# Attention chunk sums on VectorE: the three steps behind a chunk's sum are spread over the next two maxima

## Chip, cores, metric

One core of one Trainium2 chip. The metric is the device time of one execution in microseconds (us).

## What is computed

A block of three layers on x (2 batches, 256 tokens, width 256): cross attention onto a context of 4096 tokens, self attention, and a mixture of experts. The change lies in the cross attention. Its core, in the reference:

```python
qh = (q @ w_q).reshape(B, L, N_HEAD, D_HEAD).transpose(0, 2, 1, 3)
kvp = c @ w_kv
k, v = (kvp[..., :D_HEAD], kvp[..., D_HEAD:])
attn_score = jnp.einsum('bhid,bjd->bhij', qh, k) / np.sqrt(D_HEAD)
attn_prob = jax.nn.softmax(attn_score, axis=-1)
out = jnp.einsum('bhij,bjd->bhid', attn_prob, v)
out = out.transpose(0, 2, 1, 3).reshape(B, L, D)
return out @ w_concat
```

There are 16 heads of width 16, and one K and V for all of them. The context serves as both halves of the keys, so that every key counts twice, which leaves the softmax as it is over 4096 keys.

## The kernel before

The 2 x 16 x 256 rows of queries are cut into 16 chunks of 512 (two heads of one batch each); chunks 0 to 7 are batch 0. In the main loop chunk g goes through 32 steps s of 128 keys. At each step TensorE makes a block of transposed scores (line 574, into one of three banks), and ScalarE takes its exponential into Pb (line 962). Every four steps TensorE multiplies Pb with V (line 585) and adds it up in the bank ACC, whose 17th column of each head is the denominator. For the softmax the greatest score of each row is needed ahead of the exponentials: while chunk g is worked on, TensorE also makes the scores of chunk g+1 in the other orientation (line 568), 1024 keys wide, in a pair of banks pairS0 or pairS1. One pair is filled over two steps (an even one and the odd one behind it), and VectorE takes its maximum (row_max, line 1170) into mxp. After 16 pairs VectorE takes the maximum over them (mneg, line 1178), GpSimd splits it in two parts (mparts), and TensorE and ScalarE put it into qparts (the "rows" of lines 554 and 939).

The pairs are a ring of two. A turn number counts every use of it (MAX_TURN); TensorE waits ahead of turn n until max_free has counted n - 1, so until the use of two turns before is released. VectorE waits on max_filled.

The sums of chunk g - 1 take a turn of this ring, at step 12 of chunk g (SUMS_AT). ScalarE has saved ACC to SBUF; TensorE transposes it into the pair whose turn it is (line 593), and VectorE does three steps (sums_rows, lines 1184 to 1188): it adds the four quarters to osum, takes the reciprocal of the denominators (oden), and multiplies the two into O. Each of the first two is waited for by the next with the semaphore dve_chain (Chain.step), and the third one's end counts max_free up. The turn behind it is the maximum of step 12 of the same chunk, in the other pair; the turn after that, at step 14, fills again the pair that held the sums.

Other work is placed between steps by a table (BETWEEN): "qs" (the rows of queries of a later chunk, lines 545 and 546) at step 14 in chunks 6 to 13, ahead of that step's scores; and in chunks 0 to 4 the preparation of batch 1 at steps 8, 15 and 22. In chunk 2 that of step 15 is the projection of half a context (line 517), whose high part ScalarE takes (kvh) and whose low part VectorE takes (kvl, low_part, line 1165). SIDES_AT says at which steps the products with V come: step 20 and 21 have none. In chunk 15 there are no maxima left; batch 0 is closed there (close_T(0) transposes O at step 2), and batch 1 behind the loop. The sums of chunk 15 go through bank0 there (line 1258) and count o_done up, for which close_T(1) waits.

The engines run in order, each its own queue; SyncE issues all DMAs. The loop of chunks is written out by the program, without a planner.

Of the kernel before, what the change touches and what calls it, by code (L numbers as in the profile page):

```python
# [8 lines left out]
ALU = mybir.AluOpType  # L9
ACT = mybir.ActivationFunctionType  # L10
AX = mybir.AxisListType.X
# [11 lines left out]
XH, XD = 16, 16  # L23
KT = S // P
CW = 512
NCH = XH * L // CW
NBLK = CW // P
# [23 lines left out]
SUMS_AT = 12  # L51
# [10 lines left out]
NCHUNK = B * NCH  # L62
# [21 lines left out]
def pair_at(g, s):  # L84

    n = (g * KT + s) // 2
    return AHEAD_OF[n] if n < len(AHEAD_OF) else None


def turns():  # L90

    exp_turn, max_turn = {}, {}
    for what in PRO:
        ring = max_turn if what[0] == "max" else exp_turn
        ring[what] = len(ring)
    for g in range(NCHUNK):
        for s in range(KT):
            if s == SUMS_AT and g:
                max_turn["sums", g - 1] = len(max_turn)
            for what in BETWEEN.get((g, s), ()):  # L100
                exp_turn[what] = len(exp_turn)
            exp_turn["s", g, s] = len(exp_turn)
            if s % 2 == 0 and pair_at(g, s):
                max_turn[("max", *pair_at(g, s))] = len(max_turn)
    return exp_turn, max_turn


EXP_TURN, MAX_TURN = turns()
# [42 lines left out]
def build(nc, x, ctxT, w_q, w_kv, w_cat, w_qk, w_v, b_qkv, w_out, b_out, gate_wT, gate_b, w_up, w_down, out):  # L151
    with ExitStack() as stack:
# [3 lines left out]
        def sem(name):  # L156
            return stack.enter_context(nc.semaphore(name))

        bank = [stack.enter_context(nc.psum_tensor(f"bank{i}", [P, 512], F32)) for i in range(4)]
        pairS = [stack.enter_context(nc.psum_tensor(f"pairS{i}", [P, 1024], F32)) for i in range(2)]  # L160
# [47 lines left out]
        with ExitStack() as cross:  # L208
            def xb(name, shape, dt=F32):
                return cross.enter_context(nc.sbuf_tensor(name, shape, dt))  # L210
# [10 lines left out]
            osum = xb("osum", [P, NBLK, XD + 1])  # L221
# [7 lines left out]
            oden = xb("oden", [P, NBLK])  # L229
# [18 lines left out]
        max_filled, max_free = sem("max_filled"), sem("max_free")  # L248
# [8 lines left out]
        mparts_ready = sem("mparts_ready")  # L257
        pv_done = sem("pv_done")
        acc_saved, accT_ps = sem("acc_saved"), sem("accT_ps")
        o_done, oT_ps, oT_done, y_ps = sem("o_done"), sem("oT_ps"), sem("oT_done"), sem("y_ps")  # L260
        q_ps, k_ps, v_ps = sem("q_ps"), sem("k_ps"), sem("v_ps")
        q_moved, k_moved, v_moved = sem("q_moved"), sem("k_moved"), sem("v_moved")
# [193 lines left out]
        def _(pe):  # L456
            mm, tr = nc.tensor.matmul, nc.tensor.transpose

            def batch_T(src, b, dst):

                for k in range(KD):
                    for t in range(2):
                        last = tr(dst[:, k * L + t * P:k * L + (t + 1) * P],
                                  src[:, 2 * b + t, k * P:(k + 1) * P], ident[:])
                return last
# [130 lines left out]
            def close_T(b):  # L596
                if b == 0:
                    pe.wait_ge(max_free, MAX_TURN["sums", NCHUNK - 2])
                else:
                    pe.wait_ge(o_done, 1)  # L600
                batch_T(O, b, OFF[:, 0:512] if b == 0 else bank[1]).then_inc(oT_ps, 1)

            def close_product(b):
# [20 lines left out]
            for g in range(NCHUNK):  # L624
                for s in range(KT):
                    if s == SUMS_AT and g:
                        sums(g - 1, max_bank(("sums", g - 1))).then_inc(max_filled, 1)
                    if s == 2 and g == NCHUNK - 1:
                        close_T(0)
# [136 lines left out]
            sums(G - 1, bank[0]).then_inc(accT_ps, 1)  # L766
            begin_out(ACC)
            close_T(1)
            pe.wait_ge(v_moved, 2)
            attn_scores(0)  # L770
# [27 lines left out]
            n = NCYC  # L798
# [303 lines left out]
        def _(dve):  # L1102
            ch = Chain(dve, dve_chain)
# [27 lines left out]
            def close(b):  # L1131
                dve.wait_ge(y_ps, b + 1)
                add_batch(b, OFF[:, 512:1024] if b == 0 else MISC[:])
                layer_norm(range(2 * b, 2 * b + 2))

            def oT_move():
                dve.wait_ge(oT_ps, 1)
                CP(xnT[:, :, 0:L], OFF[:, 0:512].rearrange("p (k n) -> p k n", k=KD)).then_inc(oT_done, 1)

            def high(dst, full, here, done):  # L1140

                dve.wait_ge(here, 16)
                CP(dst[:], full[:]).then_inc(done, 1)
# [7 lines left out]
            def x_parts(src):  # L1151
                dve.wait_ge(xnT_ps, 1)
                CP(xh[:, :, 0:L], src.rearrange("p (k n) -> p k n", k=KD)).then_inc(xh_done, 1)
                x_low(0, src)

            def low_part(what):
                n = EXP_TURN[what]
                if what[0] == "qT":
                    m, cols = what[1], slice(what[2] * L, (what[2] + 1) * L)
                    dst, high, src = ql[:, m, cols], qh[:, m, cols], EXP[n % 3][:, 0:L]  # L1160
                else:
                    i = (2 * what[1] + what[2]) % 2
                    dst, high, src = kvl[:, i, :], kvh[:, i, :], EXP[n % 3][:]
                dve.wait_ge(exp_free, n + 1)
                TT(dst, src, high.bitcast(F32), ALU.subtract).then_inc(low_done, 1)

            def row_max(c, blk, kp):
                n = MAX_TURN["max", c, blk, kp]
                dve.wait_ge(max_filled, n + 1)
                nc.vector.reduce_max(mxp[:, c % 2 * NBLK + blk, kp:kp + 1], pairS[n % 2][:], AX).then_inc(max_free, 1)  # L1170
                if (blk, kp) == (NBLK - 1, NPAIR_K - 1):
                    block_max(c, n)

            def block_max(c, n):
                dve.wait_ge(max_free, n + 1)
                if c >= 2:
                    dve.wait_ge(mparts_ready, c - 1)
                nc.vector.tensor_reduce(out=mneg[:, c % 2, :], in_=mxp[:, c % 2 * NBLK:(c % 2 + 1) * NBLK, :],  # L1178
                                        op=ALU.max, axis=AX, negate=True).then_inc(mneg_ready, 1)

            def sums_rows(g, src, done):
                b, c = g // NCH, g % NCH
                quarters = src.rearrange("p (i k c) -> p i c k", i=NBLK, k=4)
                ch.step(nc.vector.reduce_sum(osum[:], quarters[:, :, 0:XD + 1, :], AX))
                ch.step(nc.vector.reciprocal(oden[:], osum[:, :, XD]))
                den = oden[:].rearrange("p (h t o) -> p h t o", t=2, o=1)
                dst = O[:, 2 * b:2 * b + 2, c * 2 * XD:(c + 1) * 2 * XD].rearrange("p t (h d) -> p h t d", h=2)
                TT(dst, osum[:, :, 0:XD].rearrange("p (h t) d -> p h t d", t=2), den.broadcast_to([P, 2, 2, XD]),
                   ALU.mult).then_inc(done, 1)

            dve.wait_ge(x_in, 16)
            layer_norm(range(0, 2))
# [15 lines left out]
            for g in range(NCHUNK):  # L1208
                for s in range(KT):
                    if s == 2 and g == NCHUNK - 1:  # L1210
                        oT_move()
                        for i in range(2):
                            high(wAh[i], wA[i], wA_in[i], wA_hi)
                        close(0)
                        for i in range(2):
                            high(wVh[i], wV[i], wV_in[i], wV_hi)
                    if s == 20 and g == NCHUNK - 1:
                        x_parts(OFF[:, 0:512])
                        TS(bq8[:], bqkv[:, 0, :], 1.0 / np.sqrt(AD), None, ALU.mult).then_inc(bq_done, 1)
                    if s == SUMS_AT and g:  # L1220
                        n = MAX_TURN["sums", g - 1]
                        dve.wait_ge(max_filled, n + 1)
                        sums_rows(g - 1, pairS[n % 2][:, 0:512], max_free)
                    for what in BETWEEN.get((g, s), ()):
                        if what in HALVED:
                            low_part(what)
                    if s % 2 == 0 and pair_at(g, s):
                        row_max(*pair_at(g, s))


            PJ, SB = [half[0], half[1]], [half[2], half[3]]
# [23 lines left out]
            dve.wait_ge(late_in, 16 * 6)  # L1255
            k_move(0, first, 1, PJ[1])
            dve.wait_ge(accT_ps, 1)
            sums_rows(NCHUNK - 1, bank[0][:], o_done)
            row_max(0)
            row_max(1)  # L1260
            reciprocals(0)
# [18 lines left out]
            n = NCYC  # L1280
# [161 lines left out]
```

## Time and profile before

| | us |
|---|---|
| median of 3 runs | 633.71 |
| lowest and highest | 627.2, 636.61 |
| the profiled execution | 633.59 |
| its span, first to last instruction | 631.8 |
| TensorE busy | 582.3 |
| VectorE busy | 465.1 |
| ScalarE busy | 410.4 |
| GpSimd busy | 118.3 |

PE is TensorE's matmuls, PEld its weight loads, DVE is VectorE, ACT is ScalarE, POOL is GpSimd. Times count from the start of the span. In a timeline each row has the start, the duration, the engine, the line, the operation and the tiles, output first; in brackets stands the idle time of the engine just before the row and what ended it, where there was some to tell of. Matmul ends are modelled. The chunk loop runs from about 50 to 414 us, the sums of chunk g - 1 in chunk g at 80.8 us for g = 1 to 405.5 us for g = 15; the last sums follow at 420.7 us.

### The profile page before, as it was taken

How to read it: one execution, taken by the hardware profiler on the slowest of the kernel's cores; microseconds unless marked ns; L12 is line 12 of the kernel's file. 1: busy time of each engine (PE TensorE's matmuls, PEld its weight loads, DVE VectorE, ACT ScalarE, POOL GpSimd, SP SyncE). 2: the span in 40 equal slices, each digit the busy share in tenths (PEclk: the TensorE clock that was granted, in tenths of full speed). 3: DMA queues.
4: the chain of work that ended last, by engine and by line, in shares of the span. 5: the costliest groups of instructions: out<-in, count | busy, mean ns of one | idle time of the engine just before them, and what ended most of it. 6: DMA issues, size and time to landing. Idle time of an engine off the chain costs nothing.

```text
span 631.8 us, 11892 instructions
## 1 busy us (share of the span) xinstructions
PE 582.3 (92%) x4512; PEld 322.6 (51%) x4512; DVE 465.1 (74%) x685; ACT 410.4 (65%) x834; POOL 118.3 (19%) x150
## 2 busy tenths in 40 slices
PE   3798999999999999999999998998999987789995
PEld 1363443444444444444444443466766655678885
DVE  6787887887999999899899994625545556584554
ACT  1347887888888887888888788654555540543451
POOL 4000000000000000000000001302355440357873
PEclk9999999999999999999999999899999997898998
DMA  8640001000000000000000000100001000122321
GB/s 316 245 142 1 2 1 32 37 3 1 1 2 2 1 2 1 2 2 1 1 3 1 1 1 2 34 1 1 25 26 43 17 5 5 58 84 75 100 83 34
DMA packets 11381, 21.99 MB, mean 35 GB/s; under 512 B 1858, under 2 KB 6724, under 8 KB 10308
## 3 DMA queue, kind: packets, MB, share of 16 engines
q1 hardware_dynamic: 11332, 21.31, 10.0%
q8 instruction: 34, 0.56, 0.4%
q14 instruction: 15, 0.12, 0.1%
HBM read 20.78 MB, written 0.52 MB: 34 GB/s over the span
## 4 chain that ended last, share of the span: by engine, by line
PE 73%; DVE 15%; ACT 5%; issue 4%; DMA 2%; POOL 1%; SPq 0%; DVEq 0%
PE bank L574 21%; PE bank L585 16%; DVE mxp L1170 11%; PE pairS L838 6%; PE pairS L663 5%; PE bank L855 4%; PE pairS L713 3%; ACT Pb L962 2%; PE bank L738 2%; PE bank L724 2%; PE bank L517 1%; PE pairS L824 1%; PE pairS L568 1%; DMA ctx<-ctxT 1%; PE pairS L593 1%
## 5 line engine op out<-in xcount | busy, mean ns | idle before, releaser
L1170 DVE TENSOR_REDUCE mxp<-pairS 128x1 f32<-128x1024 f32 x256 | 306.7, 1221 | 36.1 <-PE pairS L568 34.9
L962 ACT ACTIVATE Pb<-bank 128x512 f32<-128x512 f32 x512 | 274.0, 599 | 56.4 <-PE bank L574 43.8
L574 PE MATMUL bank<-qparts,kparts 64*128 64x512 f32 x512 | 189.7, 453 | 12.9 <-DVE mxp L1170 6.4
L568 PE MATMUL pairS<-kparts,qparts 64*128 64x512 f32 x512 | 189.3, 455 | 2.8 <-DVE mxp L1170 2.0
L585 PE MATMUL bank<-Pb,V 128*32 128x256 f32 x2048 | 151.6, 389 | 1.2 <-ACT accS L948 1.2
L574 PEld LDWEIGHTS bank<-qparts,kparts 64*128 64x128 f32 x512 | 78.6, 184 | 117.2 <-ACT Pb L962 75.5
L585 PEld LDWEIGHTS bank<-Pb,V 128*32 128x32 f32 x2048 | 46.5, 108 | 74.4 <-issue 47.5
L568 PEld LDWEIGHTS pairS<-kparts,qparts 64*128 64x128 f32 x512 | 78.0, 184 | 7.6 <-DVE mxp L1170 2.5
L383 POOL CAST mparts<-mneg 128x8 fp32r<-128x8 f32 x16 | 3.2, 199 | 368.6 <-DVE mneg L1178 368.6
L1241 DVE TENSOR_REDUCE smx<-pairS 128x2 f32<-128x512 f32 x32 | 21.8, 686 | 32.7 <-PE pairS L713 32.7
L398 POOL TENSOR_TENSOR Pb<-Pb,srd 128x512 f32<-128x512 f32 x32 | 33.3, 1041 | 66.6 <-DVE srd L1246 66.3
L989 ACT ACTIVATE Pb<-pairS,smx 128x256 f32<-128x256 f32 x64 | 29.7, 471 | 22.5 <-DVE smx L1241 22.5
L1306 DVE SCALAR_TENSOR_TENSOR xs<-bank,cw,xs 128x256 f32<-128x256 f32 x72 | 29.9, 478 | 8.2 <-PE bank L855 7.1
L1301 DVE TENSOR_TENSOR Pb<-pairS,Pb 128x512 f32<-128x512 f32 x18 | 12.4, 690 | 30.1 <-ACT Pb L1052 30.1
L838 PE MATMUL pairS<-xh,wAh 128*128 128x512 f32 x64 | 26.5, 414 | 2.7 <-POOL wAl L421 2.7
L1052 ACT ACTIVATE Pb<-pairS 128x512 f32<-128x512 f32 x18 | 10.7, 597 | 25.3 <-PE pairS L838 24.5
L1252 DVE COPY Pb<-bank 128x512 f32<-128x512 f32 x32 | 21.9, 684 | 6.2 <-PE bank L724 5.9
L838 PE MATMUL pairS<-xl,wAh 128*128 128x512 f32 x64 | 25.9, 405 | 0.0
L838 PE MATMUL pairS<-xh,wAl 128*128 128x512 f32 x64 | 25.6, 400 | 0.0
L421 POOL TENSOR_TENSOR hl<-Pb,hh 128x512 fp32r<-128x512 f32 x16 | 20.9, 1304 | 15.7 <-issue 6.8
L855 PE MATMUL bank<-wDh,hh 128*128 128x256 f32 x64 | 19.1, 298 | 4.1 <-POOL hl L421 4.1
L724 PE MATMUL bank<-ident,Pb 128*128 128x128 f32 x128 | 20.2, 280 | 1.8 <-DVE Pb L1252 1.8
(176 smaller groups left out, 730.5 us busy)
## 6 DMA issues: line engine op xcount, KB each, us to landing
ctx<-ctxT SPq DMA_DIRECT2D x4, 2048.0 KB, 8.4
wU<-w_up SPq DMA_DIRECT2D x18, 256.0 KB, 2.7
wD<-w_down SPq DMA_DIRECT2D x18, 128.0 KB, 2.4
wA<-w_qk SPq DMA_DIRECT2D x8, 256.0 KB, 2.7
wO<-w_out SPq DMA_DIRECT2D x8, 128.0 KB, 2.1
wV<-w_v SPq DMA_DIRECT2D x2, 512.0 KB, 3.7
xs<-x SPq DMA_DIRECT2D x2, 256.0 KB, 6.0
out<-xs SPq DMA_DIRECT2D x2, 256.0 KB, 2.2
```

Source lines behind the costliest of these rows:

```text
L398: TT(w, w, srd[:, u % 4, :].unsqueeze(2).broadcast_to([P, 2, L]), ALU.mult).then_inc(s_norm, 1)
L568: last = mm(dst[:, i * 512:(i + 1) * 512], qparts[rows, at:at + P], kparts[c // NCH][rows, k:k + 512], start=True, stop=True)
L574: mm(dst[:], kparts[g // NCH][rows, s * P:(s + 1) * P], qparts[rows, g * CW:(g + 1) * CW], start=True, stop=True).then_inc(exp_filled, 1)
L585: last = mm(ACC[32 * j:32 * j + 32, cols], V[g // NCH][:, t, :], PT[:, t % 8, cols], start=(v == 0 and side == 0), stop=(v == QUADS - 1 an ...
L663: last = mm(dst, left, right, start=(k == 0 and n == 0), stop=(k == KD - 1 and n == 2))
L724: last = tr(PTB[:, kt * L + hf * P:kt * L + (hf + 1) * P], sp_[:, u % 4, hf * L + kt * P:hf * L + (kt + 1) * P], ident[:])
L838: last = mm(dst[par], wt[:, c:c + P], xt[:, k, :], start=(n == 0), stop=(n == 3 * KD - 1))
L855: last = mm(DB[par][t // 2][:, (t % 2) * D:(t % 2 + 1) * D], ht[:, t * P:(t + 1) * P], wt, start=(n == 0), stop=(n == len(terms) - 1))
L962: A(PT[:, s % 8, :], src, ACT.Exp, scale=1.0 / np.sqrt(XD)).then_inc(exp_free, 1)
L989: last = A(sp_[:, u % 4, hf * L:(hf + 1) * L], SB[u % 2][:, hf * L:(hf + 1) * L], ACT.Exp, bias=smx[:, u % 4, hf:hf + 1], accum_out=sden[: ...
L1170: nc.vector.reduce_max(mxp[:, c % 2 * NBLK + blk, kp:kp + 1], pairS[n % 2][:], AX).then_inc(max_free, 1)
L1306: ins = nc.vector.scalar_tensor_tensor(out=xs[:, t, :], in0=DB[par][t // 2][:, (t % 2) * D:(t % 2 + 1) * D], scalar=cw[:, t, cw_e], in1=xs ...
```

## The change

The function sums_rows becomes three, and what was one block at step 12 is spread. At step 12 VectorE makes osum (sum_quarters), and the end of this step counts max_free up. Then comes the maximum of step 12, then the reciprocal (row_weights), then the maximum of step 14, and then the product into O (scale_rows). The reciprocal waits for osum by max_free, the product waits for the reciprocal by a new semaphore osum_done, and o_done now counts all 16 products, so that close_T waits for 8 or 16 of them. The last sums, behind the loop, keep the three steps one behind the other.

```diff
             def close_T(b):
                 if b == 0:
                     pe.wait_ge(max_free, MAX_TURN["sums", NCHUNK - 2])
-                else:
-                    pe.wait_ge(o_done, 1)
+                pe.wait_ge(o_done, NCH * (b + 1))
                 batch_T(O, b, OFF[:, 0:512] if b == 0 else bank[1]).then_inc(oT_ps, 1)
...
-            def sums_rows(g, src, done):
+            def sum_quarters(src, done):
+                quarters = src.rearrange("p (i k c) -> p i c k", i=NBLK, k=4)
+                nc.vector.reduce_sum(osum[:], quarters[:, :, 0:XD + 1, :], AX).then_inc(done, 1)
+
+            def row_weights(g):
+                nc.vector.reciprocal(oden[:], osum[:, :, XD]).then_inc(osum_done, 1)
+
+            def scale_rows(g):
                 b, c = g // NCH, g % NCH
-                quarters = src.rearrange("p (i k c) -> p i c k", i=NBLK, k=4)
-                ch.step(nc.vector.reduce_sum(osum[:], quarters[:, :, 0:XD + 1, :], AX))
-                ch.step(nc.vector.reciprocal(oden[:], osum[:, :, XD]))
+                dve.wait_ge(osum_done, g + 1)
                 den = oden[:].rearrange("p (h t o) -> p h t o", t=2, o=1)
                 dst = O[:, 2 * b:2 * b + 2, c * 2 * XD:(c + 1) * 2 * XD].rearrange("p t (h d) -> p h t d", h=2)
                 TT(dst, osum[:, :, 0:XD].rearrange("p (h t) d -> p h t d", t=2), den.broadcast_to([P, 2, 2, XD]),
-                   ALU.mult).then_inc(done, 1)
+                   ALU.mult).then_inc(o_done, 1)
...
                     if s == SUMS_AT and g:
                         n = MAX_TURN["sums", g - 1]
                         dve.wait_ge(max_filled, n + 1)
-                        sums_rows(g - 1, pairS[n % 2][:, 0:512], max_free)
+                        sum_quarters(pairS[n % 2][:, 0:512], max_free)
                     for what in BETWEEN.get((g, s), ()):
                         if what in HALVED:
                             low_part(what)
                     if s % 2 == 0 and pair_at(g, s):
                         row_max(*pair_at(g, s))
+                    if s == SUMS_AT and g:
+                        dve.wait_ge(max_free, MAX_TURN["sums", g - 1] + 1)
+                        row_weights(g - 1)
+                    if s == SUMS_AT + 2 and g:
+                        scale_rows(g - 1)
...
             dve.wait_ge(accT_ps, 1)
-            sums_rows(NCHUNK - 1, bank[0][:], o_done)
+            sum_quarters(bank[0][:], last_sums)
+            dve.wait_ge(last_sums, 1)
+            row_weights(NCHUNK - 1)
+            scale_rows(NCHUNK - 1)
```

VectorE's queue in chunks 1 and 2 before. The first sums here are those of chunk 0, done in chunk 1, the second those of chunk 1, done in chunk 2; the two maxima ahead of kvl are those of steps 12 and 14.

```order
L1184 TENSOR_REDUCE osum<-pairS 128x68 [waits max_filled]
L1185 RECIPROCAL oden<-osum 128x4 [waits dve_chain]
L1188 TENSOR_TENSOR O<-osum,oden 128x2x2x16 [waits dve_chain]
L1170 TENSOR_REDUCE mxp<-pairS 128x1 [waits max_filled] x6
L1178 TENSOR_REDUCE mneg<-mxp 128x4 [waits mparts_ready,max_free]
L1170 TENSOR_REDUCE mxp<-pairS 128x1 [waits max_filled] x10
L1184 TENSOR_REDUCE osum<-pairS 128x68 [waits max_filled]
L1185 RECIPROCAL oden<-osum 128x4 [waits dve_chain]
L1188 TENSOR_TENSOR O<-osum,oden 128x2x2x16 [waits dve_chain]
L1170 TENSOR_REDUCE mxp<-pairS 128x1 [waits max_filled] x2
L1165 TENSOR_TENSOR kvl<-bank,kvh 128x512 [waits exp_free]
```

The first of them is followed by six maxima in a row, and in chunk 2 kvl follows directly on a maximum. The same place in the changed kernel:

```order
L1183 TENSOR_REDUCE osum<-pairS 128x68 [waits max_filled]
L1170 TENSOR_REDUCE mxp<-pairS 128x1 [waits max_filled]
L1186 RECIPROCAL oden<-osum 128x4 [waits max_free]
L1170 TENSOR_REDUCE mxp<-pairS 128x1 [waits max_filled]
L1193 TENSOR_TENSOR O<-osum,oden 128x2x2x16 [waits osum_done]
L1170 TENSOR_REDUCE mxp<-pairS 128x1 [waits max_filled] x4
L1178 TENSOR_REDUCE mneg<-mxp 128x4 [waits mparts_ready,max_free]
L1170 TENSOR_REDUCE mxp<-pairS 128x1 [waits max_filled] x10
L1183 TENSOR_REDUCE osum<-pairS 128x68 [waits max_filled]
L1170 TENSOR_REDUCE mxp<-pairS 128x1 [waits max_filled]
L1186 RECIPROCAL oden<-osum 128x4 [waits max_free]
...
```

The sum, the reciprocal and the product now have one maximum between each two of them. Chunk 2 goes on as follows, with the product between the maximum of step 14 and kvl:

```order
L1170 TENSOR_REDUCE mxp<-pairS 128x1 [waits max_filled]
L1193 TENSOR_TENSOR O<-osum,oden 128x2x2x16 [waits osum_done]
L1165 TENSOR_TENSOR kvl<-bank,kvh 128x512 [waits exp_free]
L1170 TENSOR_REDUCE mxp<-pairS 128x1 [waits max_filled] x4
L1178 TENSOR_REDUCE mneg<-mxp 128x4 [waits mparts_ready,max_free]
```

All other chunks up to 14 are as chunk 1. In chunk 15, where no maxima are left, the three steps stand one behind the other as before. The queues of the other engines have the same instructions in the same order.

## Rows read from the trace of the kernel before

**Rows 1.** The page: busy us, share of the span, instructions.

```profile
PE 582.3 (92%) x4512; PEld 322.6 (51%) x4512; DVE 465.1 (74%) x685; ACT 410.4 (65%) x834; POOL 118.3 (19%) x150
```

**Rows 2.** Busy us by stretch: PE, PEld, DVE, ACT, POOL; PEclk, DMA, GB/s.

```profile
176.00:384.00 208.00, 203.22 (x1914) 88.98 (x1910) 189.82 (x190) 172.35 (x327) 3.70 (x18) 1.00 0.01 1
```

**Rows 3.** Groups by line, TensorE, 176 to 384 us: busy, mean ns, idle before.

```profile
L574 PE MATMUL bank<-qparts,kparts 64*128 64x512 f32 x302 | 112.9, 448 | 4.8 <-DVE mxp L1170 4.0
```

**Rows 4.** Timeline of VectorE, chunk 6, from the sum to step 22.

```profile
198.37 0.44 DVE L1184 TENSOR_REDUCE osum<-pairS 128x68 f32<-128x272 f32 x1 [0.15 <-PE pairS L593]
198.84 0.18 DVE L1185 RECIPROCAL oden<-osum 128x4 f32<-128x4 f32 x1
199.06 0.23 DVE L1188 TENSOR_TENSOR O<-osum,oden 128x64 f32<-128x64 f32 x1
199.20 1.22 DVE L1170 TENSOR_REDUCE mxp<-pairS 128x1 f32<-128x1024 f32 x1
201.05 1.23 DVE L1170 TENSOR_REDUCE mxp<-pairS 128x1 f32<-128x1024 f32 x1 [0.64 <-PE pairS L568]
202.28 1.22 DVE L1170 TENSOR_REDUCE mxp<-pairS 128x1 f32<-128x1024 f32 x1
203.52 1.22 DVE L1170 TENSOR_REDUCE mxp<-pairS 128x1 f32<-128x1024 f32 x1
204.75 1.22 DVE L1170 TENSOR_REDUCE mxp<-pairS 128x1 f32<-128x1024 f32 x1
205.89 1.21 DVE L1170 TENSOR_REDUCE mxp<-pairS 128x1 f32<-128x1024 f32 x1
```

**Rows 5.** Timeline of TensorE, chunk 6: pairs completed (L568), starts of steps 20, 22.

```profile
200.59 0.39 PE L568 MATMUL pairS<-kparts,qparts 64*128 64x512 f32 x1
...
201.82 0.39 PE L568 MATMUL pairS<-kparts,qparts 64*128 64x512 f32 x1
...
203.06 0.39 PE L568 MATMUL pairS<-kparts,qparts 64*128 64x512 f32 x1
...
203.95 0.50 PE L574 MATMUL bank<-qparts,kparts 64*128 64x512 f32 x1
...
204.89 0.47 PE L574 MATMUL bank<-qparts,kparts 64*128 64x512 f32 x1 [0.20 <-DVE mxp L1170]
```

**Rows 6.** Timeline of both engines, chunk 5, steps 12 to 14.

```profile
177.15 0.39 PE L568 MATMUL pairS<-kparts,qparts 64*128 64x512 f32 x1
...
177.51 0.23 DVE L1188 TENSOR_TENSOR O<-osum,oden 128x64 f32<-128x64 f32 x1
...
177.66 1.22 DVE L1170 TENSOR_REDUCE mxp<-pairS 128x1 f32<-128x1024 f32 x1
...
178.04 0.50 PE L574 MATMUL bank<-qparts,kparts 64*128 64x512 f32 x1
...
178.85 1.23 DVE L1170 TENSOR_REDUCE mxp<-pairS 128x1 f32<-128x1024 f32 x1
```

**Rows 7.** Timeline of both engines, chunk 2, steps 14 to 16.

```profile
108.41 1.23 DVE L1170 TENSOR_REDUCE mxp<-pairS 128x1 f32<-128x1024 f32 x1 [1.93 <-PE pairS L568]
109.55 0.68 DVE L1165 TENSOR_TENSOR kvl<-bank,kvh 128x512 fp32r<-128x512 f32 x1
...
110.38 0.47 PE L574 MATMUL bank<-qparts,kparts 64*128 64x512 f32 x1 [1.04 <-DVE kvl L1165]
```

**Rows 8.** Line 1188: durations in ns (least, median, most), who waited (us, times).

```profile
L1188 DVE TENSOR_TENSOR O<-osum,oden x16: 224/225/1710, 81.5 to 421.4; 128x64 f32<-128x64 f32 x16
...
  PEld bank L574: 2.5, 6
```

**Rows 9.** Timeline of VectorE in the self attention.

```profile
430.00 0.16 DVE L1246 RECIPROCAL srd<-sden 128x2 f32<-128x2 f32 x1
430.07 0.67 DVE L1252 COPY Pb<-bank 128x512 f32<-128x512 f32 x1
```

More of the change, by code:

```diff
@@ L259, in build @@
         acc_saved, accT_ps = sem("acc_saved"), sem("accT_ps")
+        osum_done, last_sums = sem("osum_done"), sem("last_sums")
         o_done, oT_ps, oT_done, y_ps = sem("o_done"), sem("oT_ps"), sem("oT_done"), sem("y_ps")
```

## Prediction

> **What bounds the kernel now.** I read the page's busy shares first: TensorE is busy 92% of the span, VectorE 74% [rows 1]. The change touches only the fifteen places in the chunk loop where VectorE turns the sums of a finished chunk into rows of O, so I went to that loop next. In the stretch from 176 to 384 us, which is most of chunks 5 to 14, TensorE is busy 203.2 of 208 us and VectorE 189.8 [rows 2]. That is close on both sides; either could decide. The groups of instructions by line settle it for TensorE: its idle time in this stretch is 4.8 us, and 4.0 of them end with a maximum of VectorE (line 1170) [rows 3]. So VectorE is waited for, but at its maxima, and little: at 0.2 us each it is some 20 waits in ten chunks, two a chunk. The question becomes: at which maximum does TensorE wait, and is that maximum late because VectorE was held up, or because TensorE filled its pair of banks late?
>
> The timeline of chunk 6 answers. VectorE does the sum at 198.37, the reciprocal at 198.84, the product at 199.06, the maximum of step 12 at 199.20, and then nothing until 201.05, where it waits 0.64 us for TensorE to fill the pair of step 14 [rows 4]. From there each maximum starts 0.07 us behind its fill: the matmul that completes the pair of step 16 ends at 201.82 + 0.39 = 202.21 and the maximum starts at 202.28; the one of step 18 ends at 203.06 + 0.39 = 203.45 and the maximum starts at 203.52 [rows 4, 5]. TensorE then waits 0.20 us at step 22, until 204.89, for that maximum of step 18 [rows 5]: 203.52 + 1.22 = 204.74, and 0.15 more until TensorE starts. The waiting thus rests on a fill, a maximum and a release; VectorE's own queue adds nothing to it. Where VectorE does run from its own queue, maximum follows maximum after 205.89 - 204.75 = 1.14 us, though each lasts 1.22 [rows 4]. TensorE's pace is a pair in 1.23 to 1.24 us (202.28 to 203.52), so VectorE gains about 0.09 us on it with each pair.
>
> **The early release.** The pair that held the sums is filled again at step 14. Before, it is released by the end of the product. In chunks 6 to 13 TensorE has the q rows of a later chunk to do ahead of step 14 and its completing matmul starts at 200.59 [rows 5], long after the product's end at 199.06 + 0.23 = 199.29 [rows 4]: nothing to gain. Chunk 5 has no such filler: the product ends at 177.51 + 0.23 = 177.74, with 0.15 us for the release 177.89, and TensorE starts step 14 at 178.04, with no idle time in front of it [rows 6]. That leaves 0.15 us. The waits of weight loads put 2.5 us in 6 places to the product [rows 8], one for each of the six chunks (1 to 5 and 14) without q rows ahead of step 14; but a weight load overlaps the matmuls before it, and the matmul behind it did not wait. I take the early release as 0.
>
> **The maximum of step 12, now directly behind the sum.** Before, it starts 199.20 - 198.84 = 0.36 us behind the reciprocal's start [rows 4]. Now it needs only its fill. In chunk 5 that fill ends at 177.15 + 0.39 = 177.54, so it can start at 177.61, against 177.66 before: 0.05 us [rows 6]. TensorE needs its release only for step 16, over a microsecond later. Value: 0.
>
> **The reciprocal, now between the maxima of steps 12 and 14.** In chunks 1 to 4 and 6 to 13 VectorE is idle there (0.64 us in chunk 6) and it lasts under 0.2 us: hidden. In chunks 5 and 14 VectorE is not idle: the maximum of step 12 at 177.61, the next instruction 1.14 later at 178.75, and the maximum of step 14 came at 178.85. The nearest row of a reciprocal between two instructions that it has nothing to do with is that of the attention part: 0.07 us from its start to the next start (430.00 to 430.07), out of 0.16 of its own [rows 9]. So the maximum of step 14 comes at 178.82, or at 178.91 with the whole 0.16; what it used before is 178.85. Between -0.03 and +0.06 us, and step 18 has room for it, as follows. Value: 0.
>
> **The product, now between the maxima of steps 14 and 16.** This is the one part that goes into a tight place. Before, the next maximum starts 199.20 - 199.06 = 0.14 us behind it [rows 4]; that is the value I take, the full 0.23 is the upper bound for an undisturbed one. In chunk 6: maximum of step 14 at 201.05, product at 202.19, maximum of step 16 at 202.33 in place of 202.28, maximum of step 18 not before 202.33 + 1.14 = 203.47. Its fill allows 203.52. The delay is gone before the maximum that TensorE waits for. The general form: the product may cost 203.52 - 201.05 - 2 x 1.14 = 0.19 us before anything is passed on. Step 20 needs the release of the maximum of step 16, at 202.33 + 1.22 + 0.15 = 203.70, and TensorE comes to it at 203.95 [rows 5]. With 0.14 the price is 0; with 0.23 it is 0.04 us in each of the 11 chunks (4 to 14) where TensorE waits at step 22, together 0.44. Chunks 1 and 3 have other work at steps 15 and 22 and more room.
>
> Here the Trainium skill bears on the case. Its page "VectorE: DVE Perf Modes", section "The DRAIN you can't avoid", says that the next VectorE operation does not start until the pipeline of the one before has emptied, that a semaphore costs nothing extra, and that one should cut the number of operations. By that rule the product would cost all of its 0.23 us in its new place, and the moved waits would save nothing. The trace speaks against the first half: maximum behind maximum starts 1.14 us after one that lasts 1.22, and the maximum behind the product 0.14 us after one that lasts 0.23 [rows 4]. The sum by the rule would be 0.44 + 0.23 = +0.7 us, by the rows +0.1.
>
> **The exception is chunk 2.** There ctx is projected at step 15, and VectorE makes the low part kvl behind the maximum of step 14: maximum at 108.41, kvl at 109.55, and TensorE idle 1.04 us until 110.38 for kvl [rows 7]. The product, issued at step 14, now stands between the two, and TensorE waits for all of it: +0.14 us (0.23 at most, 0.36 if the whole stretch from reciprocal to maximum is the right row).
>
> **The rest.** In chunk 15 no maxima are left, and the last sum of all (420 us) keeps its order; both keep three steps one behind the other, with other semaphores. The transposes of O for batch 0 wait for a count of 8 products, which is reached in chunk 8, and for the maxima as before. No DMA, nothing on SyncE, ScalarE or GpSimd moves. Sum: 0 + 0 + 0 + 0 + 0.14 = +0.14 us. On the profiled execution, 633.59 us (a span of 631.8 and 1.8 around it), that is 633.7; on the median of the runs shown, 633.71, it is 633.85. I say 633.8. Its own range is 633.5 (0.05 in a few places gained) to 634.4 (+0.44 + 0.23).
>
> **Rivals.** (1) *The pair was waited for after all.* For it: the 2.5 us of rows 8. If all of it came back the time would be 631.2. If the 0.36 us that the maxima move forward reached the end in all 15 chunks, 5.4 us, it would be 628.3; this is the most that the change can give, since VectorE's work itself stays. Against it: no matmul shows idle time there, and in 8 of the chunks the filler hides it anyway. Chance 0.08. (2) *Slower: the product holds up the maximum of step 18.* It decides from 0.19 us. If the product costs 0.36 in its new place (reciprocal's start to maximum's start, the nearest row of a stretch with waits in it), each of the 11 chunks loses 0.36 - 0.19 = 0.17, 1.9 us, and chunk 2 0.36: +2.2, 636.0. For it: the product carries a wait of its own in a place that is full. Against it: that wait was fulfilled a microsecond before. At the far end stands the slowest of the 16 products, 1.71 us against a median of 0.225 [rows 8]: (1.71 - 0.19) x 11 + 1.7 = +18.4, 652. Which one it is does not matter for the bound; the median says that the others do not share its length. Chance 0.07, of which 0.01 for the far end. (3) The forecast: 0.85.
>
> **How the numbers follow.** All likely cases lie within 5.4 us below and 2.2 above; the three runs shown spread from 627.2 to 636.6, more than any of them. So the range is set by the scatter about 633.8: 628.0 to 638.0. A change of over 2% (12.7 us; about what a measurement of this kernel can tell from none) follows from no case but the far end of rival 2, 0.01, and scatter gives some 0.02 on either side: faster 0.02, same 0.95, slower 0.03.
>
> **What would show it.** Right: in chunk 6 of the changed kernel the maximum of step 12 starts about 0.4 us behind the sum, the product 1.14 us behind the maximum of step 14, the next maximum 0.14 behind it, that of step 18 still 0.07 behind its fill; TensorE's idle time at step 22 stays 0.20; in chunk 2 its wait for kvl grows from 1.04 to 1.18; from the sum to the matmul behind the wait of step 22 it stays 204.89 - 198.37 = 6.52 us. Rival 1: chunks 1 to 5 and 14 get shorter. Rival 2: the wait at step 22 grows in chunks 4 to 14 alike. I am wrong if these 6.52 us move by more than 0.05, or if the gap from product to maximum is over 0.19.

## The result and the profile after

| | before | changed |
|---|---|---|
| median of 20 runs, us | 636.3 | 636.2 |
| mean of these, us | 634.7 | 636.3 |
| lowest and highest, us | 627.2, 637.9 | 631.8, 642.5 |
| profiled execution, us (its span) | 633.59 (631.8) | 636.60 (634.8) |

The comparison gives 1.0052 for the changed kernel over the one before, interval 1.0029 to 1.0075: half a percent slower, where 0.02% was forecast. The median lies inside the predicted range (628 to 638), and the class is "within 2%", but an interval that leaves out 1.000 has to be explained. The ratio leaves out runs more than 1.5% above the fastest of the same kernel, and since one run of before was as low as 627.2 this takes away 9 of its 20 and 1 of the other's 20; the means of what is left are 632.6 and 636.0, and this is the 0.5%. Of all 20 runs the means differ by 1.6 us, with a standard error of 0.9, and the medians by 0.1: half of the 3.3 us comes from what the ratio leaves out. So before looking for 3.3 us in the chunk loop one has to ask whether they are there.

The page, first, in the row that answers to [rows 1]:

```profile
PE 583.7 (92%) x4512; PEld 322.4 (51%) x4512; DVE 462.2 (73%) x685; ACT 410.3 (65%) x834; POOL 118.1 (19%) x150
```

VectorE's busy time fell by 2.9 us, although the same 685 instructions ran, while TensorE's rose by 1.4. Most of the 2.9 fit the overlap: the reciprocal now starts ahead of the end of the maximum before it (below, 204.63 against 203.49 + 1.23 = 204.72), the product too, while before each waited for the step ahead of it. It is no time that anyone waits for. What matters is where the span grew by 3.0 us. The starts of the 16 sums are good marks for that, since they come once a chunk:

| stretch | before | changed | difference |
|---|---|---|---|
| start of the span to the first sum | 80.82 | 85.04 | +4.22 |
| sum of chunk 1 to that of chunk 2 | 23.61 | 23.62 | +0.01 |
| 2 to 3 | 26.11 | 26.23 | +0.12 |
| 3 to 14 | 245.50 | 245.57 | +0.07 |
| 14 to 15 | 29.44 | 27.78 | -1.66 |
| 15 to the last sum | 15.25 | 15.24 | -0.01 |
| last sum to the end of the span | 211.1 | 211.4 | +0.3 |

The first row is more than the whole of the 3.0 us, and it lies ahead of the first instruction whose place the change moves. The stretches of the trace, 0 to 60 us and 380 to 424 us, show most of what it is. The columns are busy us and instructions of PE, PEld, DVE, ACT and POOL, then the granted clock of TensorE as a share of full speed, then the DMA share and GB/s. Before:

```profile
0.00:60.00 60.00, 42.81 (x256) 22.16 (x256) 44.75 (x75) 24.52 (x44) 7.84 (x29) 1.00 0.50 185
380.00:424.00 44.00, 40.37 (x321) 19.26 (x320) 17.42 (x39) 29.41 (x55) 8.13 (x6) 0.96 0.05 13
```

The changed kernel:

```profile
0.00:60.00 60.00, 42.52 (x212) 21.72 (x212) 41.74 (x72) 21.11 (x38) 7.78 (x29) 0.91 0.50 185
380.00:424.00 44.00, 40.36 (x346) 18.47 (x344) 20.46 (x43) 31.94 (x59) 8.13 (x6) 1.00 0.04 13
```

In the first 60 us TensorE's clock stood at its full 2.4 GHz before the change and fell to 1.2 GHz for part of the time after it (mean 0.91), and 212 matmuls were done where it had been 256. At 380 to 424 it is the other way round, 0.96 before and 1.00 after: the 1.66 us that the stretch from chunk 14 to 15 is shorter. Up to the first sum both kernels run the same instructions in the same order. The 4.22 us come in three pieces: TensorE's projection of the context begins behind its DMA at 11.53 us, before at 11.14 (0.4); its first transposed scores begin at 48.7 and 47.0 us, so 1.3 more have come by then, with a fall of the clock that lasts from 30 to 33 us; and the other 2.5 come with a fall from 50 to 57 us.

Now the place that the change was about. VectorE in chunk 6 of the changed kernel, which answers to [rows 4]:

```profile
202.71 0.44 DVE L1183 TENSOR_REDUCE osum<-pairS 128x68 f32<-128x272 f32 x1
203.49 1.23 DVE L1170 TENSOR_REDUCE mxp<-pairS 128x1 f32<-128x1024 f32 x1 [0.33 <-PE pairS L569]
204.63 0.17 DVE L1186 RECIPROCAL oden<-osum 128x4 f32<-128x4 f32 x1
205.41 1.23 DVE L1170 TENSOR_REDUCE mxp<-pairS 128x1 f32<-128x1024 f32 x1 [0.62 <-PE pairS L569]
206.56 0.21 DVE L1193 TENSOR_TENSOR O<-osum,oden 128x64 f32<-128x64 f32 x1
206.69 1.22 DVE L1170 TENSOR_REDUCE mxp<-pairS 128x1 f32<-128x1024 f32 x1
207.88 1.23 DVE L1170 TENSOR_REDUCE mxp<-pairS 128x1 f32<-128x1024 f32 x1
```

And TensorE there, the fills of steps 16 and 18 and the start of step 22, as in [rows 5]:

```profile
206.18 0.39 PE L569 MATMUL pairS<-kparts,qparts 64*128 64x512 f32 x1
...
207.41 0.39 PE L569 MATMUL pairS<-kparts,qparts 64*128 64x512 f32 x1
...
209.25 0.46 PE L575 MATMUL bank<-qparts,kparts 64*128 64x512 f32 x1 [0.21 <-DVE mxp L1170]
```

The maximum of step 12 waits 0.33 us for its fill instead of standing behind reciprocal and product; it starts 203.49 - 202.71 = 0.78 us behind the sum's start, before 0.83, so it moved forward by 0.05 us. The product starts 206.56 - 205.41 = 1.15 us behind the maximum of step 14 and the next maximum 0.13 behind the product; that maximum is 206.69 - 206.57 = 0.12 us behind the end of its fill, 0.05 later than it could be. The maximum of step 18 is again at 207.88, 0.08 behind its fill (207.41 + 0.39 = 207.80). TensorE's wait at step 22 is 0.21, before 0.20, and from the sum to the matmul behind this wait it is 209.25 - 202.71 = 6.54 us, before 6.52. The delay is gone within one maximum.

Chunk 2, which answers to [rows 7]:

```profile
112.63 1.22 DVE L1170 TENSOR_REDUCE mxp<-pairS 128x1 f32<-128x1024 f32 x1 [1.97 <-PE pairS L569]
113.77 0.21 DVE L1193 TENSOR_TENSOR O<-osum,oden 128x64 f32<-128x64 f32 x1
113.90 0.68 DVE L1165 TENSOR_TENSOR kvl<-bank,kvh 128x512 fp32r<-128x512 f32 x1
...
114.73 0.47 PE L575 MATMUL bank<-qparts,kparts 64*128 64x512 f32 x1 [1.17 <-DVE kvl L1165]
```

The product stands between the maximum and kvl, and TensorE waits 1.17 us where it had waited 1.04. This is the +0.12 of the table.

### The profile page after: what moved, and what is told of

Read it like the earlier page. It is cut to its first block, busy times and chain, and to the rows that moved or that the text cites. A ratio compares the mean times of both kernels' runs of the same rounds, so it can differ in the third digit from the quotient of the medians.

```text
span 634.8 us, 11893 instructions
## 1 busy us (share of the span) xinstructions
PE 583.7 (92%) x4512; PEld 322.4 (51%) x4512; DVE 462.2 (73%) x685; ACT 410.3 (65%) x834; POOL 118.1 (19%) x150
## 4 chain that ended last, share of the span: by engine, by line
PE 74%; DVE 14%; ACT 4%; issue 3%; DMA 2%; POOL 1%; SPq 0%; DVEq 0%
PE bank L575 21%; PE bank L586 16%; DVE mxp L1170 11%; PE pairS L838 7%; PE pairS L663 5%; PE bank L855 4%; PE pairS L713 3%; ACT Pb L962 2%; PE bank L738 2%; PE bank L724 2%; PE bank L518 2%; DMA ctx<-ctxT 1%; PE pairS L569 1%; PE pairS L594 1%; PE pairS L824 1%
```

## Experiments

Two questions: do the small terms hold, each alone and pushed until they hurt; and what are the 3.3 us of the ratio? Since an effect of a tenth of a microsecond drowns in the times of whole runs, the small ones are read from the distances between sums in each run's profile. The columns below are the first sum's start and the distances from the sum of chunk 2 to 3, 3 to 14 and 14 to 15, in us; the mean of all timed runs; their mean granted clock; and the ratio to the kernel before run beside them, with its interval. The distances are differences of starts printed to 0.01 us.

| kernel | first sum | 2 to 3 | 3 to 14 | 14 to 15 | mean us (runs) | clock | ratio |
|---|---|---|---|---|---|---|---|
| before | 80.82 | 26.11 | 245.50 | 29.44 | | | |
| changed | 85.04 | 26.23 | 245.57 | 27.78 | 636.3 (20) | 0.9752 | 1.0052 (1.0029 to 1.0075) |
| before again | 82.16 | 26.12 | 245.48 | 29.41 | 635.7 (12) | 0.9759 | 1.0017 (0.9986 to 1.0049) |
| changed again | 81.53 | 26.26 | 245.52 | 27.79 | 634.1 (12) | 0.9797 | 1.0013 (0.9976 to 1.0049) |
| changed, third | 82.03 | 26.24 | 245.49 | 27.80 | 634.6 (12) | 0.9792 | 1.0002 (0.9970 to 1.0033) |
| release only | 81.45 | 26.11 | 245.48 | 29.36 | 635.1 (12) | 0.9783 | 1.0015 (0.9984 to 1.0046) |
| kvl first | 82.41 | 26.12 | 245.52 | 27.78 | 632.9 (12) | 0.9817 | 0.9968 (0.9934 to 1.0002) |
| product x2 | 81.72 | 26.36 | 246.10 | 29.45 | 636.5 (12) | 0.9777 | 0.9978 (0.9934 to 1.0023) |
| product x4 | 81.30 | 28.00 | 248.93 | 28.11 | 641.6 (6) | 0.9737 | 1.0142 (1.0091 to 1.0193) |
| no reciprocal, no product | 83.73 | 26.11 | 245.51 | 27.78 | 633.4 (12) | 0.9796 | 0.9987 (0.9947 to 1.0026) |
| before, half a product moved | 82.98 | 26.14 | 244.08 | 29.26 | 633.6 (12) | 0.9794 | 0.9991 (0.9959 to 1.0024) |
| changed, half a product moved | 83.53 | 26.28 | 244.02 | 27.65 | 633.3 (12) | 0.9802 | 0.9966 (0.9926 to 1.0005) |

The kernel before ran beside these on the three chips used: 29 times beside the first repeats, the release alone and four products (mean 633.9), 35 times beside the third changed run, kvl first, two products and the kernel without the two steps (633.9), and 23 times beside the last two (635.4). The ratios can't tell an effect of 1 us: that of two products is below 1, though its mean is 2.6 us above that of before beside it. Only that of four products is clear of 1.

### The same kernel against itself

No edit.

> The kernel before, unchanged, against itself. Theory A (the change costs 0.1 us, and the 0.5% of the result is scatter that comes from when TensorE's clock falls): the ratio differs from 1 by as much as 0.5% here too, or its interval is as wide as that; the first sum of the chunk loop (80.8 us in the first profile, 85.0 in the changed kernel's) moves by some us from profile to profile though the code is the same; from the sum of chunk 2 to that of chunk 3 26.11 us, from there to that of chunk 14 245.5. Theory B (the change itself costs some 3 us): the ratio is 1.000 within 0.2%, and the first sum stays at 80.8.

Measured: ratio 1.0017, interval 0.9986 to 1.0049. The first sum moved from 80.82 to 82.16 us with the same code, while the distances in the loop repeat to 0.03. But the ratio itself did not move by 0.5%, only its interval reaches that far, and the 1.34 us in this profile are not the clock, which was full in its first 60 us too, with 243 matmuls where it had been 256:

```profile
0.00:60.00 60.00, 41.45 (x243) 21.43 (x244) 44.52 (x74) 23.23 (x42) 7.81 (x29) 1.00 0.50 185
```

They stem from the start: TensorE waits for the DMA of the context until 12.49 us, where it had been 11.14. So theory A holds in that there is scatter ahead of the loop, but its reason is only one of two. The mean of the 12 runs is 1.9 us above the 29 runs beside them (standard error 1.5), at a clock of 0.9759 against 0.9801. Of two identical kernels one can thus come out 1.9 us over the other.

### The changed kernel again, twice

No edit.

> The changed kernel again. Theory A: within 0.3% of the kernel before run beside it, 634 to 637 us; from the sum of chunk 2 to that of chunk 3 26.23 us (0.12 more than before), every other distance between sums up to chunk 14 within 0.03 of before's. Theory B: ratio 1.005 again, and the first sum late again at about 85.

> The changed kernel once more, to set the size of scatter. Theory A: mean of its runs within 1.5 us of the mean of before's runs beside it, in either direction, and runs of equal mean granted clock within 0.5 us of before's. Theory B: 3.3 us over, at equal clock too. Theory C (the change makes the clock fall more often, so that the cost is real but lies in the clock): over before by 1 us or more again, at a lower mean clock.

Measured: ratios 1.0013 (0.9976 to 1.0049) and 1.0002 (0.9970 to 1.0033), means 0.2 and 0.7 us over before's beside them. The 1.005 did not come again, though the intervals alone don't exclude it for the first of the two; all 24 runs together have a mean 0.5 us (standard error 0.7) above the 64 beside them, and that does leave out 3.3. The first sum stands at 81.5 and 82.0 where the theory of a real cost wanted 85. Theory C wanted 1 us or more at a lower clock. The clocks are 0.9797 and 0.9792 against 0.9801 and 0.9804, a difference no larger than its error of 0.0012, so a small cost by way of the clock stays possible. The distance from 2 to 3 is 26.26 and 26.24, the forecast 26.23 to 26.25.

All runs that came with a granted clock give a sharper comparison. Through the 99 such runs of the kernel before (the 12 above among them) a straight line of time over mean clock falls by 5.2 us for 0.01 of clock (correlation -0.94). The 44 runs of the changed kernel lie 0.03 us below this line, +-0.15 (one standard error of these runs; the line's own is 0.12); the first 20 alone, those of the result, 0.1 below, +-0.3. At equal clock the change costs nothing that can be measured (its 0.13 us are too small for this), and the first 20 runs had a low clock: 0.9752 (standard error 0.0012), where the same kernel had 0.9794 (0.0010) in its 24 repeats. The clocks of the 20 runs of before beside them are not recorded, so the result's own 0.5% can't be split this way on both sides.

### The release alone

Against the kernel before, with the three functions of the change in the place of sums_rows:

```diff
-                        sums_rows(g - 1, pairS[n % 2][:, 0:512], max_free)
+                        sum_quarters(pairS[n % 2][:, 0:512], max_free)
+                        dve.wait_ge(max_free, n + 1)
+                        row_weights(g - 1)
+                        scale_rows(g - 1)
```

> The pair is released by the sum alone, but the reciprocal and the product stay directly behind it. Theory A: nothing waits for this release, so all distances between sums are those of the kernel before, chunk 2 among them (26.11 us, since the product no longer stands ahead of kvl); total as before. Rival 1 of the prediction (the pair was waited for): chunks 1 to 5 and 14 shorter by up to 0.4 us each, 2.5 us in all.

Measured: 26.11 and 245.48, those of before; chunks 1 to 5 are 23.60, 26.11, 23.59, 22.68 and 21.54 long, before 23.61, 26.11, 23.60, 22.68 and 21.55. In chunk 5 of the changed kernel the pair of step 14 is full at 182.73 + 0.39 = 183.12, 1.95 us behind the sum's start, and before too (178.38 + 0.39 - 176.82). The early release gives nothing in chunks 1 to 5. Chunk 14, the sixth without q rows, took 29.36 us, before 29.44 and 29.41; the clock fell in it each time, so that one can't be told to better than 0.1 us. The 2.5 us that the waits of weight loads put to the product were no time on the way, as the matmul behind them told.

### kvl ahead of the product

```diff
-                    if s == SUMS_AT + 2 and g:
+                    if s == SUMS_AT + (3 if g == 2 else 2) and g:
                         scale_rows(g - 1)
```

> The changed kernel, but in chunk 2 the product comes behind kvl in place of ahead of it. Theory A (the only cost of the change is the product ahead of kvl): from the sum of chunk 2 to that of chunk 3 26.11 us again, as before the change, TensorE's wait for kvl 1.04 in place of 1.18; all other distances as in the changed kernel. If the 0.14 us comes from something else in that chunk (the release, the reciprocal's place), it stays at 26.24.

Measured: 26.12. Chunk 2, VectorE and TensorE:

```profile
109.98 1.22 DVE L1170 TENSOR_REDUCE mxp<-pairS 128x1 f32<-128x1024 f32 x1 [1.98 <-PE pairS L569]
111.12 0.68 DVE L1165 TENSOR_TENSOR kvl<-bank,kvh 128x512 fp32r<-128x512 f32 x1
111.72 0.21 DVE L1193 TENSOR_TENSOR O<-osum,oden 128x64 f32<-128x64 f32 x1
...
111.95 0.47 PE L575 MATMUL bank<-qparts,kparts 64*128 64x512 f32 x1 [1.04 <-DVE kvl L1165]
```

TensorE's wait is 1.04 again. The one cost of the change in the loop is the product's place ahead of kvl.

### Two and four products in the place of one

```diff
+                if g < NCHUNK - 1:
+                    dve.wait_ge(more_done, 3 * g)
+                    for i in range(3):
+                        TT(more[i][:].rearrange("p h (t d) -> p h t d", t=2), osum[:, :, 0:XD].rearrange("p (h t) d -> p h t d", t=2),
+                           den.broadcast_to([P, 2, 2, XD]), ALU.mult).then_inc(more_done, 1)
```

(1 in place of 3 for two products. The scratch tiles and the semaphore more_done are declared elsewhere.)

> The changed kernel with one more product ahead of each. Theory A: the place has 0.19 us of room, two products of 0.13 take 0.26 and overrun it by 0.07: distance between sums in chunks 6 to 13 22.28, from chunk 2 to 3 26.37, in all 11 x 0.07 + 0.27 = 1.0 us over before. If the edge is not at 0.19 but the step-22 wait grows gradually, the distance shows it: 22.21 (room for two) or 22.34 (none for the second).

> The changed kernel with three more products (into a scratch tile) ahead of each product in chunks 1 to 14. Each costs about 0.13 us of the queue. Theory A: the place has 0.19 us of room, so 4 x 0.13 = 0.52 overruns it by 0.33 in each of the chunks 4 to 14: distance between sums 22.21 + 0.33 = 22.54, and chunk 2 to 3 26.62; 11 x 0.33 + 0.5 = 4.1 us over before in all. If the place had no room (the product is paid in full): 22.72 a chunk and 6.2 us. If VectorE has more room than worked out: 22.21, and the time as before.

Measured: chunks 6 to 13 take 22.25 to 22.28 us with two products and 22.52 to 22.55 with four, where 22.28 and 22.54 were worked out. The room of 0.19 us is confirmed from both sides of its edge: 0.13 goes for nothing, 0.26 costs 0.06, 0.52 costs 0.33. At equal clock the runs lie 1.3 (+-0.4) and 4.4 (+-0.5) us above the line of before; worked out were 1.0 and 4.1. Chunk 6 with four products, VectorE, and the wait at step 22:

```profile
204.35 1.23 DVE L1171 TENSOR_REDUCE mxp<-pairS 128x1 f32<-128x1024 f32 x1 [0.62 <-PE pairS L570]
205.49 0.48 DVE L1197 TENSOR_TENSOR more<-osum,oden 128x64 f32<-128x64 f32 x3
205.89 0.22 DVE L1199 TENSOR_TENSOR O<-osum,oden 128x64 f32<-128x64 f32 x1
206.03 3.48 DVE L1171 TENSOR_REDUCE mxp<-pairS 128x1 f32<-128x1024 f32 x3
...
208.52 0.46 PE L576 MATMUL bank<-qparts,kparts 64*128 64x512 f32 x1 [0.40 <-ACT Pb L963]
```

The three maxima stand back to back (3.48 us in all, one each 1.13), so the maximum of step 18 ends at 206.03 + 1.13 + 1.22 = 208.38, 0.14 ahead of step 22's matmul. VectorE's queue thus is what holds here: from the sum, at 201.66, to TensorE's step 22 it takes 6.86 us where it took 6.52. The bracket names ScalarE, which came last by the records; that it is VectorE is argued from the 0.14 us, which are those of the other releases, and from the size of the delay. With two products all waits at scores (4.7 us from 176 to 384) are put to VectorE's maxima. Two things missed. Chunks 1 and 3, which were said to have more room, lost some 0.13 us each with four products, and nothing with one or two. And the distance from 2 to 3 was 28.00, not 26.62; TensorE waited 1.58 us for kvl, and the clock was down for 3.4 us in this chunk:

```profile
111.51 0.47 PE L576 MATMUL bank<-qparts,kparts 64*128 64x512 f32 x1 [1.58 <-DVE kvl L1166]
```

The wait is 0.41 longer than the 1.17 of one product, the 3 x 0.13 that were worked out; the other 1.4 us fall in with the clock. In no other profile here did the clock fall in chunk 2. Whether the longer wait brought it down, one case does not show; the median of these runs, 643.6 at a clock of 0.974, would fit it.

### Without reciprocal and product

The waits for the products are dropped with them.

```diff
-                    if s == SUMS_AT and g:
-                        dve.wait_ge(max_free, MAX_TURN["sums", g - 1] + 1)
-                        row_weights(g - 1)
-                    if s == SUMS_AT + 2 and g:
-                        scale_rows(g - 1)
```

> Reciprocal and product of chunks 1 to 15 are left out (O is set to zero once at the start), only the sum of quarters and the last chunk's three steps stay. This is the most that any placing of the two can give. Theory A: nothing but the 0.14 us of chunk 2: distances 26.11 and 22.21, the time within scatter of before (633 to 636). If VectorE's work were on TensorE's path: up to 0.36 us less a chunk, 5 us.

Measured: 26.11 and 245.51. With 15 reciprocals and products taken out altogether the chunks are as long as with them in their old place: what was moved had cost nothing there, so no place could have been better in the loop. The ratio is 0.9987 (0.9947 to 1.0026), the runs 0.8 us (+-0.3) below the line of before. The distances up to the last sum don't show these 0.8; where they are was not looked for.

### The wait at step 22 itself

```diff
-SIDES_AT = [AT_ONCE, AT_ONCE, AT_ONCE, APART, APART, AT_ONCE, APART, APART]
+SIDES_AT = [AT_ONCE, AT_ONCE, AT_ONCE, APART, APART, APART, APART, APART]
```

> The kernel before, with half of the product with V of steps 20 to 23 moved from step 23 to step 21, as at its neighbours. Theory A (the wait of step 22 is a fill, a maximum and a release, and TensorE comes too early there because steps 20 and 21 have no product): the 0.20 us of idle time at step 22 goes, TensorE's work stays, so the distance between sums is 22.21 - 0.20 = 22.01 in chunks 6 to 13, and 2 us less in all. Rival: the same idle time comes back at another maximum or exponential of the chunk, since VectorE and ScalarE are nearly as full: distance 22.21, time as before.

> The same in the changed kernel. Theory A: as in the kernel before with this edit, plus the 0.14 us of chunk 2: the order of the three steps matters no more than without it. If VectorE has become the bound by then (its 189.8 of 208 us and the rest of the chunk shorter), the changed order, which takes 0.3 us less of its queue between sum and the third maximum, is the shorter one by up to that a chunk.

Measured: a chunk takes 22.05 to 22.08 us in both, 0.14 less than 22.21, and the distance from 3 to 14 is 1.4 us shorter in the one and 1.5 in the other. TensorE in the first of the two, from 176 to 384 us, against the 4.8 and 4.0 of [rows 3]:

```profile
L574 PE MATMUL bank<-qparts,kparts 64*128 64x512 f32 x304 | 113.8, 448 | 2.7 <-DVE mxp L1170 1.9
```

Half of the waits are gone, those of step 22 (9 of at most 0.2 us are left, the ones at step 2). Of the 0.20 us 0.14 were gained; the missing 0.06 was not traced. The order of the three steps makes no difference here either: 244.08 and 244.02. Both kernels are the shortest in the loop, but as whole runs the ratios are 0.9991 (0.9959 to 1.0024) and 0.9966 (0.9926 to 1.0005): a gain of 1.5 us stays inside the scatter of 12 runs.

## Why the prediction was right and wrong

*The early release, 0.* Right in chunks 1 to 13: the release alone changes no distance there. For chunk 14 the clock hides what there is below 0.1 us.

*The maximum of step 12 and the reciprocal, 0.* Right in value. In chunk 5, where VectorE was said to be busy, the distance is 21.55 us before and 21.54 with the release alone, and the trace of the changed kernel gives 21.55; the maximum of step 14 starts there at 183.19, 0.07 behind its fill, so the reciprocal at 183.07 fitted into a gap of 0.12. One sign was wrong: the maximum of step 12 was to start about 0.4 us behind the sum and starts 0.78 behind it. The prediction took off all of reciprocal and product and forgot the fill, which it had worked out itself for chunk 5 as 0.05 us. Rival 1's 0.36 us a chunk was too high for the same reason.

*The product between the maxima of steps 14 and 16, 0, with 0.19 us of room.* Right, and the best-tested step: 0.13 from its start to the next, room used up between one product and two, and 22.28 and 22.54 us, as worked out, beyond it. Four products of 0.22 us take 206.03 - 205.49 = 0.54 us of the queue, 0.135 each. The Trainium skill (page "VectorE: DVE Perf Modes", section "The DRAIN you can't avoid") says that the next operation waits for an empty pipeline, and, which the prediction left out, that "A next op that is not held starts earlier". The trace shows such earlier starts wherever the operation does not wait for the one directly ahead, and the +0.7 us worked out from the first sentence alone did not come.

*Chunk 2, +0.14.* Right in place and size: 0.12, 0.15 and 0.13 us in three profiles, and 0.01 with kvl ahead of the product.

*The rivals.* Both were tested away: rival 1 by the release alone, and by the kernel without the two steps, which is no shorter in the loop; rival 2 by its own edge, which one product does not reach. Its far end had no ground: the product of 1.71 us is the one at 406.15 us, in chunk 15, and not in one of the eleven chunks (the changed kernel has it at 408.93).

*How the numbers follow.* This is the step that failed. It took the scatter from three runs of before, as something that lies about 633.8 on both sides alike and would show as a wide range and as no difference. It has a cause that can be read, TensorE's clock, and the cause can lie unevenly on two sets of 20 runs. In the profile, with the late start of the context's projection, it is 4.2 us ahead of the first sum, 30 times the whole sum of the prediction. The median of 636.2 is 2.4 us over the forecast, yet that of before has moved just as far, from 633.7 to 636.3. The prediction put at nothing a term that is larger than all of its others: what the clock takes in the first 60 us and around 396, with both of its levels as bounds. Over whole runs it is 5.2 us for 0.01 of mean clock, and the changed kernel's mean clock was 0.9752 in these 20 runs and 0.9794 in the repeats, which is 2.2 us; the profile of before, with 1.00 up to 60 us, was at the good end of it, and no row of it said so. That the 3.3 us are no cost of the moved steps themselves is shown by the repeats (0.5 us, standard error 0.7), by the distances and by the runs at equal clock. That the clock was low in those 20 runs by chance, and not because of the change, is the likely reading and not shown: what the clock was in the 20 runs of before stays open, and half of the 3.3 us is what the ratio leaves out.

## What to carry to other kernels

Where a queue keeps pace with its producer (1.14 us a piece against 1.23), work it up as room: the idle time that comes together until the next place where somebody waits is what an inserted instruction may cost, and an instruction counts there with the distance to the next start, not with its duration. Moving steps off a place where nobody waited gains nothing, and it puts them ahead of something else; look at what it is in each chunk, since the only loss here was in the one chunk that differs. And before explaining half a percent, cut the span at marks that both traces have: a difference that is complete ahead of the first changed instruction is not the change's.

## What the runs showed of the hardware

The times of the kernel before spread from 627 to 650 us at identical code, and go with TensorE's mean granted clock: 5.2 us for each 0.01 of it. In the profiles it falls for some 3.4 us or a multiple, at places that differ; one fall of 3.4 us makes the way from chunk 14 to 15 29.4 us long in place of 27.8. It falls between 23 and 58 us in ten of the twelve (not in the two of the unedited kernel before), at 396 us in four of four profiles with the three steps together (the 29.3 to 29.4 us from chunk 14 to 15) and in none of the six with one product spread or four nor in the one without the two steps, but in the one with two products (29.45). That looks like a pattern, but in four of the seven profiles without it the clock fell at about 430 us instead, and the runs with a clock beside them (0.9801 and 0.9804 before, 0.9797 and 0.9792 changed) are too near each other to tell. Whether the order of the steps has a part in where the clock falls was not tested. The clock is not the only source: TensorE's projection of the context waits for its DMA until 11.14 us in one profile of the kernel before and until 12.49 in the other, and the first sum moves with it by 1.34 us.
